# A cross-attention and ternary FFN layer on one core: VectorE splits the feature weights before, not after, it scales the biases and masks

## The reference, cut to what matters

```python
q = heads(layernorm(x), Wq, bq); k = heads(ctx, Wk, bk); v = heads(ctx, Wv, bv)
q_prime = relu(einsum('bhnd,fd->bhnf', q, Wqf))
k_prime = relu(einsum('bhnd,fd->bhnf', k, Wkf)) * attention_mask
kv = einsum('bhnf,bhne->bhfe', k_prime, v)
out = einsum('bhmf,bhfe->bhme', q_prime, kv) / (q_prime . sum(k_prime) + 1e-8)
x = x + (out @ Wo.T + bo)
h = layernorm(x)
x = x + bit_linear(subln(bit_linear(h, w_up) * relu(bit_linear(h, w_gate))**2), w_down)
```

## Time and profile before

| | |
|---|---|
| runs | 401.2, 401.83, 403.06 us (median 401.83) |
| profiled execution | 401.2 us, of which the span from first to last instruction is 399.4 |
| granted TensorE clock | 1.000 |
| PE busy | 380.7 us (95%) |
| PEld busy | 186.6 us (47%) |
| DVE busy | 345.7 us (87%) |
| ACT busy | 316.1 us (79%) |
| POOL busy | 245.0 us (61%) |
| chain that ended last, by engine | PE 52%, DVE 29%, ACT 6%, issue 6% |

### The profile page before, as it was taken

How to read it: one execution, slowest core, us unless ns; L and a number is a source line. 1 busy time by engine, 2 the same in 40 slices (tenths; PEclk the granted TensorE clock), 3 DMA queues, 4 the chain that set the end, 5 groups by cost and what they waited for, 6 DMA issues and landing times.

```text
span 399.4 us, 8241 instructions
## 1 busy us (share of the span) xinstructions
PE 380.7 (95%) x2880; PEld 186.6 (47%) x2898; DVE 345.7 (87%) x709; ACT 316.1 (79%) x446; POOL 245.0 (61%) x224
## 2 busy tenths in 40 slices
PE   7997999999998999999999999998999999999986
PEld 2454545454555544556545444443444433444432
DVE  3968977898898998898968999999999999997983
ACT  5586877789788979987888778968879777989870
POOL 2093739895048965277267874756867666878650
PEclk9999999999999999999999999999999999999999
DMA  7898939761639722767721332344435134444265
GB/s 245 254 233 272 409 114 263 121 144 54 149 110 246 105 82 49 200 176 107 238 107 35 76 37 54 67 93 92 94 71 114 34 62 91 94 93 108 66 131 158
DMA packets 90905, 52.39 MB, mean 131 GB/s; under 512 B 78832, under 2 KB 78832, under 8 KB 90736
## 3 DMA queue, kind: packets, MB, share of 16 engines
q1 hardware_dynamic: 90864, 51.87, 52.1%
HBM read 28.78 MB, written 4.19 MB: 83 GB/s over the span
## 4 chain that ended last, share of the span: by engine, by line
PE 52%; DVE 29%; ACT 6%; issue 6%; POOL 2%; DMA 2%; DVEq 1%; SPq 0%; ACTq 0%; POOLq 0%
PE ps L1365 36%; PE ps L1430 9%; DVE amax L1240 4%; PE ps L1447 3%; DVE xq L1600 3%; DVE w L1235 2%; DVE var L1260 2%; POOL fl L864 2%; DVE fh L1235 2%; DVE fl L1092 2%; PE ps L1413 2%; ACT w L1007 1%; DVE top L1251 1%; PE ps L1397 1%; DMA area<-in_ctxT 1%
## 5 line engine op out<-in xcount | busy, mean ns | idle before, releaser
L1430 PE MATMUL ps<-tern,area 128*128 128x512 bf16 x503 | 113.9, 379 | 4.7 <-DVE w L1235 2.7
L1430 PEld LDWEIGHTS ps<-tern,area 128*128 128x128 bf16 x512 | 48.8, 98 | 66.2 <-DVE w L1235 5.2
L864 POOL TENSOR_TENSOR v<-w 128x512 f32<-128x512 f32 x32 | 41.1, 1289 | 34.4 <-DVE w L1235 34.3
L864 POOL TENSOR_TENSOR fl<-fh,w 128x512 f32<-128x512 f32 x32 | 40.9, 1290 | 18.4 <-DVE fh L1235 18.4
L1365 PE MATMUL ps<-xT,w 128*128 128x512 f16 x192 | 43.3, 379 | 2.7 <-DVE fl L1092 2.7
L996 ACT ACTIVATE w<-ps 128x512 f32<-128x512 f32 x64 | 37.2, 581 | 9.5 <-PE ps L1430 9.5
L1365 PE MATMUL ps<-w,oT 128*128 128x512 f16 x192 | 44.0, 379 | 0.0
L1092 DVE SCALAR_TENSOR_TENSOR fl<-ps,fh 128x512 f16<-128x512 f32 x64 | 40.4, 682 | 3.7 <-ACT fh L902 3.6
L1000 ACT ACTIVATE qkT<-w 128x512 f32<-128x512 f32 x64 | 40.3, 630 | 2.0
L1365 PE MATMUL ps<-ctxh,w 128*128 128x512 f16 x128 | 40.1, 379 | 1.2 <-DVE ctxl L1080 1.2
L902 ACT ACTIVATE fh<-ps 128x512 f16<-128x512 f32 x64 | 33.8, 600 | 5.4 <-PE ps L1413 4.0
(11 more groups left out here) (167 smaller groups left out, 906.0 us busy)
## 6 DMA issues: line engine op xcount, KB each, us to landing
tern<-in_wffn SPq DMA_DIRECT2D x24, 512.0 KB, 4.7
out<-o SPq DMA_DIRECT2D x16, 256.0 KB, 3.4
area<-in_ctxT SPq DMA_DIRECT2D x3, 1024.0 KB, 5.3
xs<-in_x SPq DMA_DIRECT2D x3, 1024.0 KB, 9.8
oT<-in_wkT SPq DMA_DIRECT2D x4, 256.0 KB, 5.3
area<-in_ctxT SPq DMA_DIRECT2D x4, 256.0 KB, 5.9
fh<-in_wvT SPq DMA_DIRECT2D x4, 256.0 KB, 6.7
xs<-in_x SPq DMA_DIRECT2D x4, 256.0 KB, 7.4
```

The source lines that it names most:

```text
L864: nc.gpsimd.tensor_tensor(actg[s % 2][:, q], acts[s % 2][:, q], subln[:, q], ALU.mult)\
L1430: mm = nc.tensor.matmul(acc, xqT[:, s % XT, k, :], weights[k][:, 512 * c:512 * c + 512], start=(k == 0), stop=(k == KC - 1))
```

## The change

In the start-up list of VectorE the low part of the feature weights (`featl`, with its wait for `feat_high`) now stands directly behind the scalar work of the first normalisation. The four operations on biases and masks, with their wait for `small_in`, come behind it. Nothing else in the program changes; the operations themselves are the same.

```diff
             first_stats(0)
             first_ln(0)
+            dve.wait_ge(feat_high, 1)
+            nc.vector.scalar_tensor_tensor(out=featl[:, :, :], in0=featf, scalar=F_SCALE, in1=feath[:, :, :],
+                                           op0=ALU.mult, op1=ALU.subtract).then_inc(feat_ok, 1)
+
             dve.wait_ge(small_in, 5 * 16)
             nc.vector.tensor_scalar(bqk[:, :, :], bqk[:, :, :], W_SCALE, None, ALU.mult).then_inc(bias_ok, 1)
             nc.vector.tensor_scalar(bvb[:, :, :], bvb[:, :, :], KV_DOWN, None, ALU.mult).then_inc(bias_ok, 1)
             link(nc.vector.tensor_scalar(maskh[:, :], masks[:, :], W_SCALE, None, ALU.mult))
             nc.vector.scalar_tensor_tensor(out=maskl[:, :], in0=masks[:, :], scalar=W_SCALE, in1=maskh[:, :],
                                            op0=ALU.mult, op1=ALU.subtract).then_inc(bias_ok, 2)
-            dve.wait_ge(feat_high, 1)
-            nc.vector.scalar_tensor_tensor(out=featl[:, :, :], in0=featf, scalar=F_SCALE, in1=feath[:, :, :],
-                                           op0=ALU.mult, op1=ALU.subtract).then_inc(feat_ok, 1)
-
             dve.wait_ge(bias_ok, 4)
             for m in range(KC):
                 low_k(0, m)
```

## The result

The changed kernel takes 405.03 us (median of 15 runs, 403.68 to 406.35) against 403.0 us (median of 15, 401.2 to 403.69) for the kernel before: a ratio of 1.0055, 95% interval 1.0041 to 1.0069. That is 2.0 us more. The forecast was 402.6, with 404.2 as its upper end. Two things were wrong: the loss is 1.8 to 2.0 us and not 0.8, and the base was too low. Two of the three runs shown ahead of the prediction (401.2 and 401.83, the median) are among the three fastest of the fifteen; with more runs before is at 403.0.

What follows compares the result with a forecast made beforehand. TensorE was taken as the bound, its 2.72 us wait before the first query product hanging on ACT and DVE. ACT's key tile at 24.1 us, 0.8 past its room, added to 401.83 gave 402.6 us; range 401.2 to 404.2.

Steps and rivals of the forecast that it cites:

- the base: Time of the kernel before, to which the loss was added: 401.83 us, the median of three executions.
- An earlier featl is worth nothing: On DVE, featl waits for feath from ACT and still starts at 20.60 us; gain nothing.
- The four operations wait for POOL: On DVE behind featl, bqk and maskh each wait for a POOL operation, bvb slips ahead; ACT starts at 24.1 us.
- maskl goes first: On DVE, maskl is asked for at 23.85 us, ahead of POOL's 23.88, and ends at 24.0.
- the lost turn: On DVE, maskl comes behind POOL's 1.13 us operation and ends at 25.05 us; chance 0.10.
- Rival 2: On DVE, maskl loses one turn to POOL; ACT starts at 25.15 us, cost 1.8 us, time 403.7; chance 0.10.
- The room up to 23.31 us: ACT's first key tile may start until 23.31 us harmlessly; each later microsecond delays the first query product at 33.51 equally.
- POOL's side is hidden: POOL is held up at most 0.3 us; the last transpose lands at 32.6, 0.9 us ahead of the query product.
- Nothing is given back: Behind 33.51 us TensorE works in one piece and later waits shift alike, so all 0.8 us is kept.
- rival 3: On DVE, bvb also loses its turn to POOL; ACT starts at 26.2 us, cost 2.9 us, time 404.7; chance 0.10.

Runs made afterwards that it cites:

- e1: Changed kernel with the four small operations reordered to maskh, bvb, bqk, maskl, and a semaphore replacing the maskh-to-maskl link; 402.87 us, ratio 1.0006.
- e2: Changed kernel with ACT and DVE waiting for bqk alone ahead of the first key tile, the other three waited for later; 402.45 us, ratio 1.0003.
- e6: Changed kernel plus sixteen extra TensorE products on zeros between the values and key features of group 0; 404.03 us, ratio 1.0037.
- e3: Changed kernel plus eight extra TensorE products on zeros between the values and key features of group 0; 405.09 us, ratio 1.0061.
- e8b: Changed kernel with POOL starting its first x tile only after the four small operations have ended; 404.4 us, ratio 1.0046.
- e0: The kernel before, run again with no edit; 403.17 us, ratio 1.0017.

## Why the prediction was wrong, point by point

- **An earlier featl is worth nothing.** Right: it started as soon as feath was ready, at 20.85, as in before relative to `shift` (1.63 against 1.62 us).
- **The four operations wait for POOL.** Right, and bqk (1.12), bvb (0.28, asked for 0.02 ahead of POOL) and maskh (1.01) went nearly as written.
- **maskl goes first.** This is the step that failed. I put it 0.03 us behind the end of maskh and 0.03 ahead of POOL. It comes 0.11 behind, and lost to POOL by 0.06. The 0.11 stood in the trace of before: maskh ended at 19.33 + 0.17 = 19.50 (its row is below the list), and maskl started at 19.61. I had taken the 0.03 from other pairs of the trace instead of from this pair. A turn is worth 1.15 us (e1), and I let it hang on a number that I had not read; 0.10 was the chance that I gave to the lost turn. Rival 2 says what happened: key tile at 25.15 on the clock of that profile, and 25.39 - (19.22 - 18.98) = 25.15 is what came.
- **The room up to 23.31 us.** Right as a sum for ACT (e2), and as a one-for-one loss behind it. Wrong in what it was measured from. In the order of before the value tile is set by TensorE: `shift` came at 18.98, 18.84, 19.05 and 20.00 us in the four profiles with that order and the query product at 33.51, 33.90, 33.87 and 33.92, without regard to it. In the changed order the product follows `shift`: 19.22, 19.34 and 19.98 (changed, e6, e3) gave 35.61, 35.72 and 36.38, always 16.4 us behind. The mean of `shift` over the eleven profiles is 19.35. So the product comes at 35.7 on average, against a mean of 33.8 with the old order: 1.9 us. The profile that I worked from was early at both ends, with `shift` 0.37 and the product 0.3 us ahead of their means. The two nearly cancel: rival 2's 1.8 us on that profile is 0.1 short of the 1.9. But late arrivals, which the old order hid, now reach the end.
- **POOL's side is hidden.** Right: e2 has it, and its query product is on time (33.68 against a mean of 33.8). e8b used up that room and more.
- **Nothing is given back.** Right: 2.1 us at the query product in the profile, and e6 carries 2.2 us from 33.51 to 35.72 into its span (401.6 against 399.4).
- **The base.** Wrong. Three runs and one profile at 1.000 stood for a kernel whose usual execution has a lowered clock and takes 403.1 us. The clock row that I listed as 1.000 without a word was the rare case. With the right base the forecast would have read 403.8, still 1.2 us under the result, and rival 2 404.8.
- **The DRAIN rule of rival 3.** The Trainium skill (VectorE: DVE Perf Modes, section "The DRAIN you can't avoid") says that the next operation waits until the pipe has emptied, which I read as behind the end of the last; the same paragraph adds that a next operation that is not held starts earlier, which I left out. The rows show the earlier start: bvb is asked for at 22.92, bqk ends at 23.01. That 0.09 us is what won bvb its turn.

The row of maskh in before, from the timeline of DVE, which stands right ahead of maskl's in the earlier trace rows:

```profile
19.33 0.17 DVE L1130 TENSOR_SCALAR maskh<-masks 128x16 f16<-128x16 f32 x1
```

## What to carry to other kernels

Each of the four small operations on VectorE cost its own 0.2 to 0.3 us while GpSimd was silent; beside a train of GpSimd operations each one can cost a whole GpSimd operation, so put it ahead of the train, or make only its reader wait for it. When a forecast hangs on who asks first, read the gap of that very pair, and if it is within 0.1 us give the lost turn at least the same chance. And before summing against one profiled execution, ask what else varies from run to run: which load arrives when, and which clock was granted.

## What the runs showed of the hardware

- Where VectorE's operation and GpSimd's met, they were served in the order of their recorded starts, down to differences of 0.01 to 0.06 us: bvb at 22.92 went ahead of POOL's 22.94 (in e1 at 23.07 ahead of 23.08), maskl at 24.24 behind its 24.18.
- Not every small operation meets. In the trace of before a 128x1 one took its plain 0.15 us though POOL's had begun 0.08 us ahead of it. What sets it apart from the four was not tested:

```profile
128.69 0.15 DVE L1193 TENSOR_SCALAR wmean<-wmean 128x1 f32<-128x1 f32 x1
```
```profile
128.61 1.16 POOL L758 TENSOR_TENSOR xn<-xn 128x512 f16<-128x512 f32 x1
```

- An operation that waits on a link to the operation directly in front (maskl on maskh) was asked for 0.10 to 0.12 us behind its end in all ten profiles that have the pair; the links in the scalar work of the first normalisation take 0.03 to 0.04. The changed kernel's chain shows a separate step of the DVE queue (0.02 us) in between. Why this pair has it was not looked into.
- In the kernel before, the 2.4 GHz level of TensorE was lost behind one idle stretch of 2.7 us in 23 of 34 executions, and the 120 products behind it took 9.94 us (e0) in place of 8.25. Four products of 0.2 us in an earlier place, which left 1.9 us of idle, prevented it in 12 of 12.
